# Graph attention with 8 heads on one core: the adjacency matrix cast to bfloat16 in DRAM once, and the mask chunks loaded from that copy by the sync queue

## What is computed

```
h = relu(layernorm(x))
adj = max(adj, eye)                                  # every node sees itself
q, k, v = h @ Wq[head], h @ Wk[head], h @ Wv[head]   # 8 heads, [4096, 64] each
scores = (q @ k.T) / 8 + 0.01 * eye - 1e16 * (1 - adj)
out = x + sum over heads of softmax(scores) @ v @ Wo[head]
```

## Time and profile before

| | |
|---|---|
| runs | 2872.68, 2875.03, 2880.84 us, median 2875.03 |
| profiled execution | 2880.15 us, its span 2878.4 us |
| PE busy | 94% |
| DVE busy | 78% |
| ACT busy | 64% |
| POOL busy | 52% |
| mean busy share of DMA engines | about 0.56 |
| mean granted TensorE clock | 0.979 |

### The profile page before, as it was taken

How to read it: one execution, slowest core, us unless ns; L and a number is a source line. 1 busy time by engine, 2 the same in 40 slices (tenths; PEclk the granted TensorE clock), 3 DMA queues, 4 the chain that set the end, 5 groups by cost and what they waited for, 6 DMA issues and landing times. The chain is left out here.

```text
span 2878.4 us, 58579 instructions
## 1 busy us (share of the span) xinstructions
PE 2703.1 (94%) x17344; PEld 1907.5 (66%) x17344; DVE 2237.4 (78%) x3833; ACT 1843.9 (64%) x3041; POOL 1494.5 (52%) x2706
## 2 busy tenths in 40 slices
PE   7999999999999999999898999999999999999997
PEld 5666666666666676666655766666676666667664
DVE  6778787887787788878657877777887787888784
ACT  4566666766666676666545666666666666666664
POOL 2255565546555454656324555655545565554553
PEclk9999999999999999999999999999999999999999
DMA  5256665556566555656435555666556565654653
GB/s 157 75 137 144 135 155 128 130 133 145 138 140 151 131 132 126 150 133 150 127 97 117 122 141 131 151 137 140 137 124 143 128 154 137 139 137 120 145 133 101
DMA packets 258750, 384.95 MB, mean 134 GB/s; under 512 B 98432, under 2 KB 119424, under 8 KB 258688
## 3 DMA queue, kind: packets, MB, share of 16 engines
q0 software_dynamic: 107520, 218.26, 33.7%
q1 hardware_dynamic: 148992, 161.76, 22.3%
q10 hardware_dynamic: 2176, 4.19, 0.4%
HBM read 169.87 MB, written 12.71 MB: 63 GB/s over the span
## 5 line engine op out<-in xcount | busy, mean ns | idle before, releaser
L665 DVE CUSTOM_DVE_ANT_0 S<-psS,B 128x1024 f32<-128x1024 f32 x1024 | 1221.8, 1216 | 475.3 <-PE psS L408 239.0
L266 POOL DMA_DIRECT2D S<-S x2048 | 1006.0, 500 | 1074.5 <-DVE S L686 1031.8
L552 ACT ACTIVATE S<-S,negm 128x1024 f32<-128x1024 f32 (+1 forms) x768 | 1096.8, 1428 | 20.0 <-DVE negm L672 19.9
L559 ACT ACTIVATE PT<-psT 128x512 f32<-128x512 f32 x1024 | 607.0, 593 | 631.6 <-PE psT L421 619.8
L408 PE MATMUL psS<-K,QH 128*128 128x512 f32 x2048 | 737.0, 441 | 58.6 <-DVE mx L665 56.2
L421 PE MATMUL psT<-ident,S 128*128 128x128 f32 x4096 | 644.2, 281 | 7.3 <-ACT S L552 4.9
L408 PE MATMUL psS<-K,QL 128*128 128x512 f32 x2048 | 649.9, 399 | 0.0
L421 PEld LDWEIGHTS psT<-ident,S 128*128 128x128 f32 x4096 | 485.9, 142 | 247.3 <-issue 154.6
L686 DVE STREAM_TRANSPOSE S<-S 128x2048 f32<-128x2048 f32 x256 | 590.4, 2307 | 1.6 <-PE psO L444 0.9
L444 PE MATMUL psO<-S,V 128*64 128x256 f32 x4096 | 512.6, 394 | 74.9 <-DMA S<-S 74.8
L431 PE MATMUL psO<-PT,V 128*64 128x256 f32 x4096 | 521.8, 386 | 0.0
(11 more groups left out here) (51 smaller groups left out, 991.1 us busy)
## 6 DMA issues: line engine op xcount, KB each, us to landing
S<-S SPq DMA_DIRECT2D x2048, 64.0 KB, 2.7
S<-S POOLq DMA_DIRECT2D x2048, 64.0 KB, 2.5
B<-in_adj POOLq DMA_DIRECT2D x256, 256.0 KB, 6.6
hq<-hT_scratch SPq DMA_DIRECT2D x32, 256.0 KB, 3.5
RB<-rden_scratch SPq DMA_DIRECT2D x128, 64.0 KB, 3.3
S<-in_x SPq DMA_DIRECT2D x8, 512.0 KB, 3.6
hT_scratch<-S ACTq DMA_DIRECT2D x8, 512.0 KB, 4.4
acc<-in_x POOLq DMA_DIRECT2D x16, 256.0 KB, 7.5
```

What stands on the lines that cost most here:

```text
L266: pool.dma_start(dst, src).then_inc(late_sent[q], 16)
L552: nc.scalar.activation(part, part, ACT.Exp, bias=negm[:, h % 2, q:q + 1], accum_out=sums[:, h % 2, q, e:e + 1]).then_inc(probs_ready, 1)
L559: nc.scalar.activation(PT[:, s % RING, :], psT[s % 2][:, :], ACT.Copy).then_inc(pt_act, 1)
L665: nc.vector.tensor_tensor_reduce(out=part, in0=psS[j % 2][:, :], in1=B[:, q, k * SLOT:(k + 1) * SLOT], scale=SCALE, scalar=LOWEST, op0=ALU ...
```

## The change

A DRAM tensor `adj16` [4096, 4096] bfloat16 is added. In the first head group, POOL issues DMAs that cast adj chunks from DRAM to DRAM, two at the end of every step (four in each of the first two steps), for the block one or two ahead; block 0 isn't cast. The bias chunks of blocks 1 to 15 are loaded from `adj16` in both groups, without a cast, by SP and no longer by POOL, at these places of step h = 2: (0,0) (0,1) between SP's moves of q = 0 and of q = 1, (0,2) (0,3) (1,0) (1,1) after the moves of q = 1, and (1,2) (1,3) after the read of `RB`. In the first group SP waits ahead of them for all casts of that block. On POOL the converts stay in h = 2, with nothing between them, and converts (1,2) (1,3) of step h = 3 are put between the moves of q = 0 and those of q = 1. Block 0 is loaded from `adj` by POOL as before (`load_first`). POOL's block 14 is written out of the loop.

```
     def step(i, h, nxt, nxt2, prev):              # SP
+        move_late(i, h, 0)
+        if adj_step:
+            if norm:
+                sp.wait_ge(cast, i * (16 * SLOTS) + 16 * SLOTS)
+            for k in range(2):
+                load_adj(i + 1, 0, k)
+        move_late(i, h, 1)
+        if adj_step:
+            for k in range(2, SPT):
+                load_adj(i + 1, 0, k)
+            for k in range(2):
+                load_adj(i + 1, 1, k)
         sp.wait_ge(den_ready, count(i, h, 1, 1))
...
         sp.dma_start(RB[:, :], ...).then_inc(rden_in, 16)
+        if adj_step:
+            for k in range(2, SPT):
+                load_adj(i + 1, 1, k)
...
+    def load_adj(i, q, k):                        # SP
+        sp.wait_ge(slot_masked, count(i, 0, SLOTS, q * SPT + k + 1 - SLOTS))
+        rows = adj16[bass.ds(i * QW + q * P, P), k * SLOT:(k + 1) * SLOT]
+        sp.dma_start(B[:, q, k * SLOT:(k + 1) * SLOT], rows).then_inc(adj_in[q][k], 16)
...
+    def cast_adj(i, q, k):                        # POOL
+        at = (bass.ds(i * QW + q * P, P), slice(k * SLOT, (k + 1) * SLOT))
+        pool.dma_start(adj16[at], adj[at]).then_inc(cast, 16)
...
     def step(i, h, more, prev, own_slot, casts):  # POOL
         move_late(i, h, 0)
-        if adj_step:
-            for k in range(2):
-                load_adj(i + 1, 0, k)
+        if adj_rest:
+            for k in range(2, SPT):
+                convert(i + 1, 1, k, own_slot)
         move_late(i, h, 1)
-        if adj_step:
-            for k in range(2, SPT):
-                load_adj(i + 1, 0, k)
...
         if adj_step:
-            for half_ in range(2):
-                for k in (2 * half_, 2 * half_ + 1):
-                    convert(i + 1, 0, k, own_slot)
-                for k in (2 * half_, 2 * half_ + 1):
-                    load_adj(i + 1, 1, k)
+            for k in range(SPT):
+                convert(i + 1, 0, k, own_slot)
             for k in range(2):
                 convert(i + 1, 1, k, own_slot)
-        if adj_rest:
-            for k in range(2, SPT):
-                convert(i + 1, 1, k, own_slot)
+        if norm:
+            for block, c in casts:
+                cast_adj(block, *divmod(c, SPT))
```

More of the change, by code:

```diff
@@ L81, in wait_apart, with group_programs @@
     engine.sem_inc(passed, 1)
-def group_programs(nc, sem, g, before, x, hT, adj, Wk, Wq, Wv, Wo, base, result, t):
+def group_programs(nc, sem, g, before, x, hT, adj, adj16, Wk, Wq, Wv, Wo, base, result, t):
     (K2, V, S, B, PT, QH, QL, hq, wq, wo, O, Oodd, RB, acc, res, ident, notI, diag, mx, negm, sums, den, rden,
@@ L111, in group_programs @@
     late_sent = [sem(f"late_sent{g}{q}") for q in range(QT)]
+    adj_first = [[sem(f"adj_first{g}{q}{k}") for k in range(SPT)] for q in range(QT)]
     adj_in = [[sem(f"adj_in{g}{q}{k}") for k in range(SPT)] for q in range(QT)]
+    cast = sem(f"cast{g}")
     (bias_conv, bias_ready, q_proj, q_hi, q_lo, scores_ready, slot_masked, row_ready, probs_ready,
@@ L218, in sync_program, with move_late @@
         sp.sem_inc(rden_stored, 16 * START)
-        def step(i, h, nxt, nxt2, prev):
[L222 to L226, removed]
+        def load_adj(i, q, k):
+            sp.wait_ge(slot_masked, count(i, 0, SLOTS, q * SPT + k + 1 - SLOTS))
+            rows = adj16[bass.ds(i * QW + q * P, P), k * SLOT:(k + 1) * SLOT]
+            sp.dma_start(B[:, q, k * SLOT:(k + 1) * SLOT], rows).then_inc(adj_in[q][k], 16)
+        def move_late(i, h, q):
+            sp.wait_ge(late_transposed, count(i, h, QT, q + 1))
+            for qi, qj in SP_MOVES:
+                src, dst = late_blocks(h, q, qi, qj)
+                sp.dma_start(dst, src).then_inc(late_moved[q], 16)
+        def step(i, h, nxt, nxt2, prev):
+            more = not (isinstance(i, int) and i == PAIRS - 1)
+            adj_step = more and h == GROUP - 2
+            move_late(i, h, 0)
[10 more added lines that the diff above has]
+                    load_adj(i + 1, 1, k)
             sp.wait_ge(den_ready, count(i, h, 1, 1))
@@ L231, in step @@
             sp.dma_start(RB[:, :], rden_scratch[h % 2].rearrange("p q -> (p q)").partition_broadcast(KD)).then_inc(rden_in, 16)
-            more = not (isinstance(i, int) and i == PAIRS - 1)
+            if adj_step:
+                for k in range(2, SPT):
+                    load_adj(i + 1, 1, k)
             if h == 1 and more:
@@ L239, in gpsimd_program, with load_first @@
     def gpsimd_program(pool):
-        def load_adj(i, q, k, first=False):
-            if first and not norm:
+        def load_first(q, k):
+            if not norm:
                 pool.wait_ge(slot_masked_before, SLOTS * STEPS + q * SPT + k + 1 - SLOTS)
[L244 to L247, removed]
+            rows = adj[q * P:(q + 1) * P, k * SLOT:(k + 1) * SLOT]
+            pool.dma_start(B[:, q, k * SLOT:(k + 1) * SLOT], rows).then_inc(adj_first[q][k], 16)
+        def cast_adj(i, q, k):
+            at = (bass.ds(i * QW + q * P, P), slice(k * SLOT, (k + 1) * SLOT))
+            pool.dma_start(adj16[at], adj[at]).then_inc(cast, 16)
         def convert(i, q, k, own_slot):
-            wait_apart(pool, adj_in[q][k], i * 16 + 16, pool_passed)
+            if isinstance(i, int) and i == 0:
+                pool.wait_ge(adj_first[q][k], 16)
+            else:
+                wait_apart(pool, adj_in[q][k], i * 16, pool_passed)
             part = B[:, q, k * SLOT:(k + 1) * SLOT]
@@ L297, in gpsimd_program @@
             for k in range(SPT):
-                load_adj(0, q, k, True)
+                load_first(q, k)
         if norm:
@@ L306, in gpsimd_program, with step @@
         load_base(0)
-        def step(i, h, more, prev, own_slot):
+        def step(i, h, more, prev, own_slot, casts):
             adj_step, adj_rest = more and h == GROUP - 2, more and h == GROUP - 1
             move_late(i, h, 0)
-            if adj_step:
-                for k in range(2):
-                    load_adj(i + 1, 0, k)
+            if adj_rest:
+                for k in range(2, SPT):
+                    convert(i + 1, 1, k, own_slot)
             move_late(i, h, 1)
-            if adj_step:
-                for k in range(2, SPT):
-                    load_adj(i + 1, 0, k)
             if prev and h == 1:
@@ L323, in step, with casts @@
             if adj_step:
-                for half_ in range(2):
-                    for k in (2 * half_, 2 * half_ + 1):
-                        convert(i + 1, 0, k, own_slot)
-                    for k in (2 * half_, 2 * half_ + 1):
-                        load_adj(i + 1, 1, k)
+                for k in range(SPT):
+                    convert(i + 1, 0, k, own_slot)
                 for k in range(2):
                     convert(i + 1, 1, k, own_slot)
-            if adj_rest:
-                for k in range(2, SPT):
-                    convert(i + 1, 1, k, own_slot)
+            if norm:
+                for block, c in casts:
+                    cast_adj(block, *divmod(c, SPT))
+        def casts(i, h):
+            return [(i + 1 if h < 2 else i + 2, 2 * ((h + 2) % GROUP) + c) for c in range(2)]
         for h in range(GROUP):
-            step(0, h, True, False, 0)
+            step(0, h, True, False, 0, [(1, 4 * h + c) for c in range(4)] if h < 2 else casts(0, h))
         for own_slot in range(SPT):
-            with pool.Fori(max(1, OWN_EVERY * own_slot - 1), OWN_EVERY * (own_slot + 1) - 1) as i:
+            with pool.Fori(max(1, OWN_EVERY * own_slot - 1), min(OWN_EVERY * (own_slot + 1) - 1, PAIRS - 2)) as i:
                 for h in range(GROUP):
-                    step(i, h, True, True, own_slot)
+                    step(i, h, True, True, own_slot, casts(i, h))
         for h in range(GROUP):
-            step(PAIRS - 1, h, False, True, 0)
+            step(PAIRS - 2, h, True, True, SPT - 1, casts(PAIRS - 2, h) if h < 2 else [])
+        for h in range(GROUP):
+            step(PAIRS - 1, h, False, True, 0, [])
         store(PAIRS - 1)
@@ L832, in build @@
         for g in range(GROUPS):
-            program, before = group_programs(nc, sem, g, before, x, hT, adj, Wk, Wq, Wv, Wo, x if g == 0 else partial,
+            program, before = group_programs(nc, sem, g, before, x, hT, adj, adj16, Wk, Wq, Wv, Wo, x if g == 0 else partial,
                                              out if g == GROUPS - 1 else partial, tiles)
```

1 line of the change is left out of this document (added).

## The result

The changed kernel takes 2925.8 us (median of 4 runs, 2918.21 to 2927.87) against 2877.94 us before: a ratio of 1.0148, 95% interval 1.0127 to 1.0169. It is slower by 1.5%; 2775 us, a gain, was forecast. The profiled execution took 2918.21 us with a span of 2916.4, 38 us more than that of before.

What follows compares the result with a forecast made beforehand. Bound: late moves in h = 2, the step with eight loads, losing 5.25 and 5.73 us per block. Second group -69, first -38, opening +5: -102 us from 2880.15, 2778; median 5 less, taken as 2775, range 2730 to 2840.

Steps and rivals of the forecast that it cites:

- The price of a load: One new bfloat16 load takes 0.9 us of all 16 DMA engines, bounds 0.75 and 1.03; eight take 7.2 us.
- 9.6 in 12 us: First 12 us of h = 2: moves (7.8) and loads (0,0) (0,1) (1.8 us) fit in the DMA engines' time.
- +0.6 us for h = 2: Two loads between SP's moves make its last move late, costing the step 0.6 us, bounds 0 and 2.6.
- SP's queue behind the moves: In h = 2, loads, sums' store and RB read behind SP's moves cost nothing, with 1 to 2 us of slack.
- Converts between the moves of h = 3: On POOL they delay its last move: +0.5 us per block in both groups, bounds 0 and 1.2.
- Casts, h = 0: First group, two casts issued at T + 8.6 beside SP's last moves: +0.5 us per block, bounds 0 and 2.
- Casts, h = 3: First group, casts ending h = 2 stand in POOL's ring ahead of h = 3's moves: +1.0 us, bounds 0 and 3.
- The opening: Four casts in each of the first two steps and POOL's extra written-out block per group: together +5 us.
- (c): Rival: DRAM-to-DRAM casts at 3.3 us each hold h = 0 and h = 3, eating the first group's gain; 2810 to 2866; chance 0.17.
- (d): Rival: loads ahead of SP's q = 1 moves make them land 4 us late as before; 2866 to 2884 us; chance 0.04.
- (e): Rival: a DRAM-to-DRAM cast is slow, over 7.6 us, and the kernel gets slower, 2990 us at 8.5; chance 0.07.
- The signs: Prediction wrong if first-group blocks stay at 83 or more, or second-group h = 2 above 23 or h = 3 above 21 us.

Runs made afterwards that it cites:

- run 7: The changed kernel with SP's loads (0,0) (0,1) between its moves cut from 1024 to 64 columns: 2869.82 us median, 2876 us in the profiled execution.
- run 1: The changed kernel with SP's loads (0,0) (0,1) put behind its moves of q = 1: 2902.99 us.
- run 3: The changed kernel with the converts of h = 3 put back behind the moves of q = 1: 2906.75 us.
- run 5: The changed kernel with SP's loads behind all moves (two before the sums' store, six after), h = 3 converts behind the moves, no casts in h = 2: 2879.02 us.
- run 6: As run 5, but with the casts at their old places, two at the end of each step: 2952.35 us.
- run 8: The kernel before with its float32 loads (0,0) (0,1) on POOL moved behind the moves of q = 1: 2885.07 us.
- run 4: The changed kernel with casts of block 1 only, all blocks loading that block's rows and masks of blocks 2 to 15 left out: 2872.39 us.
- run 10: The kernel before, first group also storing finished bfloat16 bias, second loading it on POOL without converts or waiting for SP's moves: 2837.05 us, ratio 0.9867.
- run 11: As run 5, but with six loads ahead of the sums' store and two behind the read of RB: 2856.89 us.

## Why the prediction was wrong

- **What bounds the kernel** was read rightly: the late moves of the step with loads, once per block, 5.25 and 5.7 us. Run 7 brings that step to 20.4 us by taking bytes away alone.
- **The price of a load** (0.9 us of all 16 engines) was right: eight new ones take 7.1 us of DMA time in the second group's h = 2. So was that of a cast: 1.9 to 2.0 us measured (its packets in h = 0 and h = 1), 2.0 taken.
- **The step that failed: "9.6 in 12 us", the load's effect on the moves.** I divided the work by a window as if the engines could fill it. A clean step has 0.74 to 0.87 in the middle of that window and the moves keep a pace of 215 to 264 GB/s; the sum over 12 us said nothing on that. With it fell the sentence that the loads' 1.8 us of transfers "run out long before the last move is issued": the last move lands 3.8 us after its issue ended, not 1.5. The term was +0.6 us for h = 2; it is 23.3 - 19.6 = +3.7 in the second group and +4.4 in the first, some 100 of the 140 us between the forecast of -102 and the measured +38. Of the +3.7, 2.9 are the 0.5 MB between SP's moves (23.3 with, 20.4 without, run 7), 0.8 the two issues and the rest. The upper bound of 2.6, the old wait of PE, was a wait and not the length that the step gains.
- **SP's queue behind the moves** cost nothing, but not by the slack of 1 to 2 us that I had given it. Its last load is out at T + 20.5 in the mean of the second group; the step that was forecast ends at T + 20.2. It was free in time since the step took 23.3. In run 7, whose h = 2 takes 20.4 us, the spare time is 0.15 us in the mean of the second group and none in the first, and in run 1 SP is 1.1 us late.
- **Converts between the moves of h = 3**: +0.5 forecast with bounds 0 and 1.2, +1.0 measured (run 3: 20.69 to 19.68).
- **Casts, h = 0**: +0.5 per block, bounds 0 and 2, for an issue at T + 8.6. Measured: 4.7 and 7.7 us at T + 8.5, in blocks 1 and 2, and none in blocks 3 to 13, where POOL is at T + 10. The mean (+0.95) hides both. Here I had set a page's rule beside it by which the 0.5 was nearer 0.2 (the Trainium skill, DMA: Bandwidth & Descriptors, Queues, rings and completion order: an engine serves its rings in turn, a packet at a time). The measured hold is on the other side of my value, by nine times and more, and from 207 to 211 us POOL's queue has 85.9% of the engines' time and SP's 12.1%: whatever the turns are, they are not short and equal.
- **Casts, h = 3** (put in POOL's ring at the end of h = 2): +1.0 forecast, measured 22.28 - 20.69 = +1.6 per block, and 6 us when the queue is later still (runs 5 and 6). The opening was +5 and is +9.4 for block 0 and +4 between the groups; what the last 4 are isn't settled (100.8 us between the groups after 96.7; run 8, without a cast, has 99.8). In block 0 the casts at T + 8.5 of h = 1 are 6.5 us of it and h = 3 is 7.4, against a gain of 4.8 in h = 2.
- **The rivals**: (c), casts eating the first group's gain, was the one that came, with more weight: the casts cost about 50 us (run 4). It ended at 2840 because its second group still gained 38 us; that group gained 12. (d), that the moves behind the loads in SP's ring land as late as before, had the right place; I gave it 0.04. Neither (c) nor (d) alone makes the kernel slower, both together do, and I had priced no such sum. (e), slow casts, didn't happen: two of them take 3.6 to 4.5 us of the engines.
- **The signs**: of the three that I had named, two came, first-group blocks at 83 or more (86.5) and h = 2 above 23 us in the second group (23.3); h = 3 above 21 there didn't (20.7). The 80.9 us per block that I gave for the first group is 81.1 by my own terms.

## What to carry to other kernels

A mean share of a step says nothing on whether a transfer fits: take the windows of the stretch in which the transfers that somebody waits for are under way, and count the price of every byte put ahead of the last of them as delay: 1.8 us of loads held it by 2.2 us, 3.9 us of casts by 3.8. Where moves are issued by two queues, the window ends with the slower queue's last move, and a transfer that the faster queue issues when it is done is still early. Better than moving a transfer out of the way was to make its result once: run 10, which stores the finished bias in the first group and loads it in the second, with neither casts nor converts, beats both kernels, at 2837 us, 1.3% under the one before (ratio 0.9867).

## What was not expected of the hardware

- Two casts from DRAM to DRAM issued at T + 8.5 lengthen the step by 4.7 and 7.7 us and the same two at T + 10 by nothing. The casts, in another queue, take 85.9% of the engines' time for 4 us while SP's last moves wait.
- Loads behind the 1 KB store of the sums in SP's ring landed 6.3 to 7.5 us after their issue, ahead of it 4.1 to 5.3 (runs 5 and 11, second group; the loads behind are also later in the step, so that the store alone is the cause is not shown).
- A wait of PE of 3.04 us at 2290.57 us left the granted clock at 1.00, one of 2.63 us, after one of 1.15, was followed by 0.50; over the second group the changed kernel's clock is 0.99.
